# Attention mask: from bf16 matmuls on TensorE to additions by VectorE in PSUM, with the score banks made in the other order

## The chip, the cores and the metric

The kernel runs on one core of one Trainium2 chip. The metric is the device time of one execution, in microseconds (us). The core has TensorE (matmuls, PE in the profile; its weight loads are PEld), VectorE (DVE), ScalarE (ACT), GpSimd (POOL), and SyncE (SP), which issues the transfers here. Each engine works through its own instructions in order and waits on semaphores for the others.

## The reference

A macaron block on x of 4 batches x 1024 tokens x 128 features, all float32: a half-weighted feed-forward (layer norm, gate and up projections, silu, down projection), then attention with 16 heads of 64, then the same feed-forward again. The attention is what matters here:

```
h = silu(x @ W1.T + b1) @ W2.T + b2
q, k, v = split(h @ Wg.T + bg)            # 16 heads of 64
dots = (q @ k.T) * 64 ** -0.5             # per batch and head: 1024 x 1024
mask = j >= i + 64                        # query i sees keys below i + 64
dots = where(mask, -inf, dots)
out = softmax(dots) @ v  ->  @ Wo.T + bo
```

## The kernel before

The two feed-forwards stand at the ends. Between them the attention loop runs 32 turns (`TURNS`): 4 batches by 8 pairs of heads. A turn has 8 steps, c = 0 to 7. Each step handles 128 queries of both heads of the pair ("A" and "B"). The order of the query blocks is written out by hand: `at_step = [0, 7, 2, 6, 1, 5, 3, 4]`. Query block q sees keys 0 to q*128+191, so the widths of the score tiles by step are 192, 1024, 448, 960, 320, 832, 576 and 704: narrow and wide steps alternate.

PSUM has 8 banks of 512 float32 per partition. Banks 0 and 1 hold head A's scores, banks 2 and 3 head B's (`SCORE = (0, 2)`); there is only one such set, so the scores of step c+1 can't be written before both exponentials of step c have read theirs. Banks 4 and 5 take transposed probabilities, bank 6 the attended values and their output projection, bank 7 the projections of q, k and v for this or the next turn.

What one step c does, by engine, in each engine's own order:

- TensorE: `score(c)` (three float32r terms per bank and head; the two heads use two halves of the array); `turns_of(tc, ti, (0, 1))`, the first two groups of transposes of the probabilities of the step three before (`T_LAG = 3`; a group is up to four 128x128 transposes into bank 4 or 5, the even groups into 4, the odd ones into 5); one projection into bank 7 (steps 1 and 2 v, 3 and 4 k, 5 and 6 q); in steps 1, 3, 5 and 7 `attend`, the product with v of a pair of query blocks; in steps 0, 2, 4 and 6 `output`; then transposes of groups 2 and 3; then `masks` of the next step. In steps 0, 4 and 6 there are four groups, in steps 1 and 2 three, elsewhere two or one.
- `masks(c+1)` first waits until both exponentials of step c are done (`exped`, event "B"). It then writes, with bf16 matmuls (`ident16` against a piece of `mask16`), the value -3.0e38 onto the keys that the triangle at the right end of the tile hides, 128 or 64 wide, two matmuls in each step and four in step 6, where the piece crosses a bank. These matmuls open the accumulation group (`start=True`) and `score` adds to it.
- VectorE: `row_max(c)`, one maximum over the row for each head, each waiting for `scored` of its head; `take(tc, 1)`, a copy of transposed group 1 to SBUF; in steps 1 and 2 the copy of v; `take(tc, 3)` where there is a group 3; `invert(c)`, the reciprocal of the sums, which waits for the exponentials; in steps 0, 2, 4 and 6 `add_output`; in steps 3 to 6 `queries_keys_low`, the low part of k or q.
- ScalarE: `take(tc, 0)`, the two exponentials `exps(c)`, `take(tc, 2)`, in steps 1, 3, 5 and 7 `attention_out`, in steps 3 to 6 the high part of k or q (`queries_keys`).
- GpSimd multiplies the probabilities by the reciprocals (`normalise`).

Group 3 of the transposes waits until VectorE has copied group 1 of the same step out of bank 5 (`taken[1]`). The projection in step 4 waits until ScalarE and VectorE have read step 3's from bank 7 (`misc_read`).

Of the kernel before, what the change touches and what calls it, by code (L numbers as in the profile page):

```python
# [13 lines left out]
P = 128  # L14
# [22 lines left out]
def macaron(nc, x, w1t, b1, w2t, b2, wqkvt, bqk, bv, wot, bo, wgatet, wupt, wdownt, out):  # L37
# [37 lines left out]
    DOWN = 0  # L75
    WORK = 7

    def mask_pieces(c):

        lo, hi = at_step[c] * P + WINDOW, width[c]  # L80
        cuts = [lo] + [b for b in (BANK,) if lo < b < hi] + [hi]
        return [(a // BANK, a % BANK, a - lo, b - a) for a, b in zip(cuts, cuts[1:])]

    with ExitStack() as ctx:
        def sb(name, shape, dt=F32):
            return ctx.enter_context(nc.sbuf_tensor(name, shape, dt))
# [2 lines left out]
            return ctx.enter_context(nc.semaphore(name))  # L89

        ident = sb("ident", [P, P])
        ident16 = sb("ident16", [P, P], BF16)
        mask16 = sb("mask16", [P, P], BF16)
        w1_sb = sb("w1_sb", [P, P])
        w2_sb = sb("w2_sb", [P, P])
        b1_sb = sb("b1_sb", [P, 1])
# [61 lines left out]
        def phase(name, lns):  # L158
# [21 lines left out]

        T = lambda n, ev, step=1: Tally(sem(n), ev, step)
        by_head = [f"{c}{h}" for c in range(STEPS) for h in HEADS]
        scored = T("scored", by_head)
        maxed = T("maxed", by_head)
        exped = T("exped", by_head)
        inverted = T("inverted", range(STEPS))
# [14 lines left out]

        credits = {
            "sync": [slots],
            "vector": [maxed, inverted, taken[1], v_done, wo_added, qk_done],
            "scalar": [exped, taken[0], attn_out, qk_high],
            "tensor": [scored, turned, attended, proj, wo_done],
            "gpsimd": [normed],
# [96 lines left out]
        @block.gpsimd  # L304
        def _(pool):
            give_credits(pool, "gpsimd")
            nc.gpsimd.memset(ident[:], 0.0).then_inc(gp_const, 1)
            nc.gpsimd.memset(mask16[:], 0.0).then_inc(gp_const, 1)
            nc.gpsimd.memset(mhalf[:], -0.5).then_inc(gp_const, 1)
            pool.wait_ge(gp_const, 3)  # L310
            nc.gpsimd.affine_select(out=ident[:], in_=ident[:], compare_op=ALU.not_equal, fill=1.0, base=0,
                                    pattern=[[-1, P]], channel_multiplier=1).then_inc(gp_const, 1)

            nc.gpsimd.affine_select(out=mask16[:], in_=mask16[:], compare_op=ALU.is_ge, fill=MASKED, base=-1,
                                    pattern=[[-1, P]], channel_multiplier=1).then_inc(gp_const, 1)
            pool.wait_ge(gp_const, 5)
            nc.gpsimd.tensor_copy(ident16[:], ident[:]).then_inc(gp_const, 1)
            pool.wait_ge(gp_const, 6)

            def rstd_of(ph, ln, t):  # L320
                done(pool, ph.stat[ln], f"a{CT - 1}", t)
                done(pool, ph.norm[ln], "n3", t - 3)
                pool.sem_inc(idle, 1)
                nc.gpsimd.tensor_scalar(veps[ln][:], mv[ln][t % 3][:, :, 1], EPS, None, ALU.add).then_inc(ph.rstd[ln].sem, 1)
                done(pool, ph.rstd[ln], "e", t)
                nc.gpsimd.tensor_tensor(rstd[ln][t % 3][:], veps[ln][:], mhalf[:], ALU.pow).then_inc(ph.rstd[ln].sem, 1)

            def layernorm(ph, t):
                done(pool, ph.rstd["ln1"], "r", t)
                done(pool, ph.tr["ln1"], "t", t - 2)  # L330
                pool.sem_inc(idle, 1)
                for k in range(CT):
                    nc.gpsimd.tensor_scalar(xn["ln1"][t % 2][:, k, :], xres[:, t * CH + k * D:t * CH + (k + 1) * D], mv["ln1"][t % 3][:, k, 0:1],
                                            rstd["ln1"][t % 3][:, k:k + 1], ALU.subtract, ALU.mult).then_inc(ph.norm["ln1"].sem, 1)

            def add_bias(t):
                if t == 0:
                    pool.wait_ge(bo_done, 2)
                done(pool, pa.norm["ln2"], "n3", t)
                here = xres[:, chunk(t)].rearrange("p (k d) -> p k d", d=D)  # L340
                nc.gpsimd.tensor_tensor(here, here, bo_all[:].unsqueeze(1).to_broadcast([P, CT, P]), ALU.add).then_inc(pa.biased.sem, 1)

            def feed_forward(ph):
                for t in range(3):
                    rstd_of(ph, "ln1", t)
                    if t < 2:
                        layernorm(ph, t)
                if ph is pa:
                    for c in range(STEPS):
                        if width[c] < blocks[c] * P:  # L350
                            for h in range(2):
                                nc.gpsimd.memset(probs[c, h][:, width[c]:], 0.0).then_inc(zeroed, 1)
                for t in range(CHUNKS + 2):
                    if ph is pa and 0 <= t - 2 < CHUNKS:
                        rstd_of(pa, "ln2", t - 2)
                    if t + 2 < CHUNKS:
                        layernorm(ph, t + 2)
                    if ph is pa and 0 <= t - 2 < CHUNKS:
                        add_bias(t - 2)
                    if t + 3 < CHUNKS:  # L360
                        rstd_of(ph, "ln1", t + 3)

            feed_forward(pa)

            def normalise(c, i):
                pool.wait_ge(inverted.sem, inverted.after(c, i))
                pool.sem_inc(idle, 1)
                for h in range(2):
                    here = probs[c, h][:, 0:width[c]]
                    nc.gpsimd.tensor_scalar(here, here, recips[:, c, h:h + 1], None, ALU.mult).then_inc(normed.sem, 1)  # L370

            with pool.Fori(0, TURNS) as i:
                for c in range(STEPS):
                    normalise(c, i)

            feed_forward(pd)
# [116 lines left out]
        def _(dve):  # L493
# [75 lines left out]

            def row_max(c, i):  # L570

                for h in range(2):
                    dve.wait_ge(scored.sem, scored.after(f"{c}{HEADS[h]}", i))
                    src = banks[:, SCORE[h]:SCORE[h] + 2, :].rearrange("p b n -> p (b n)")[:, 0:width[c]]
                    nc.vector.tensor_reduce(negmax[:, c, h:h + 1], src, AX.X, ALU.max, negate=True).then_inc(maxed.sem, 1)  # L575

            def invert(c, i):

# [93 lines left out]
        def _(pe):  # L672
# [86 lines left out]
                    if ph is pa and 0 <= t - 2 < CHUNKS:  # L759
                        inner(t - 2)  # L760

            pe.wait_ge(gp_const, 6)
            feed_forward(pa)

            def misc_read(job, n):
# [14 lines left out]
                    last = mm(banks[:, ATTEND, (2 + b) * P:(3 + b) * P], attn[:, j, b * P:(b + 1) * P], w, start=True, stop=True)  # L780
                last.then_inc(wo_done.sem, 1)

            def masks(c, i):

                pe.wait_ge(exped.sem, exped.after(*(lambda t, s: (f"{s}B", t))(*back(i, c, 1))))
                for h in range(2):
                    for b, col, m0, w in mask_pieces(c):
                        mm(banks[:, SCORE[h] + b, col:col + w], ident16[:], mask16[:, m0:m0 + w], start=True, stop=False, skip_group_check=True)  # L788

            def score(c, i, r):  # L790

                masked = {b for b, _, _, _ in mask_pieces(c)}
                if c < 2:
                    pe.wait_ge(qk_done.sem, qk_done.after(("q0", "q1")[c], i))
                edges = list(range(0, width[c], BANK)) + [width[c]]
                for b, (a, z) in enumerate(zip(edges, edges[1:])):
                    terms = ((0, 0), (0, 1), (1, 0))
                    for n, (sq, sk) in enumerate(terms):
                        for h in range(2):
                            last = mm(banks[:, SCORE[h] + b, 0:z - a], qt[r][sq][half(h), at_step[c] * P:(at_step[c] + 1) * P], kt[r][sk][half(h), a:z],  # L800
                                      start=n == 0 and b not in masked, stop=n == 2, skip_group_check=True)
                            if z == width[c] and n == 2:
                                last.then_inc(scored.sem, 1)

            def turn(c, g, i):

# [35 lines left out]
                    if g < groups[c]:  # L842
                        turn(c, g, i)

            def step(c, i, r, carry=True, more=True, final=False):

                ti, tc = back(i, c, T_LAG)
                turning = carry or c >= T_LAG
# [6 lines left out]
                if c in JOBS and runs(job, carry, more):  # L855
                    k = JOB_ORDER.index(job)
                    name, t = (JOB_ORDER[k - 1], i) if k else (JOB_ORDER[-1], i - 1)
                    misc_read(name, job_turn(name, t))
                    project(job, job_turn(job, i), 1 - r if job_turn(job, 0) else r)
                if attending:  # L860
                    attend(ATTEND_AT[c], *((i, r) if c >= PV_LAG else (i - 1, 1 - r)))
                if c in OUTPUTS and runs(OUTPUTS[c], carry, more):
                    output(OUTPUTS[c], job_turn(OUTPUTS[c], i))
                if turning:
                    turns_of(tc, ti, (2, 3))
                if not (final and c == STEPS - 1):
                    n, s = (i, c + 1) if c + 1 < STEPS else (i + 1, 0)
                    masks(s, n)

            pe.wait_ge(pa.h.sem, pa.h.after("h", CHUNKS - 1))  # L870
            pe.wait_ge(pa.x1.sem, pa.x1.after("x", CHUNKS - 1))
            pe.wait_ge(zeroed, 2 * sum(width[c] < blocks[c] * P for c in range(STEPS)))
            pe.wait_ge(qk_done.sem, qk_done.after("k0", 0))
            project("q1", 0, 0, 4)
            masks(0, 0)
            for c in range(STEPS):
                step(c, 0, 0, carry=False)
            with pe.Fori(0, TURNS // 2 - 1) as i2:
# [2 lines left out]
                for c in range(STEPS):  # L881
                    step(c, i2 * 2 + 2, 0)
            for c in range(STEPS):
                step(c, TURNS - 1, 1, more=False, final=True)
            for c in range(PV_LAG):
                if c < T_LAG:
                    turns_of(c + STEPS - T_LAG, TURNS - 1, (0, 1, 2, 3))
# [36 lines left out]
```

## Time and profile before

| what | value |
|---|---|
| time, median of 3 runs | 1389.04 us (1388.59 to 1392.15) |
| the profiled execution's own time | 1391.63 us |
| its span | 1389.7 us |
| granted TensorE clock, mean | 0.993 of full speed |
| TensorE busy | 1346.3 us, 97% |
| VectorE busy | 869.5 us, 63% |
| ScalarE busy | 827.7 us, 60% |
| GpSimd busy | 1041.3 us, 75% |

Busy time is the time covered by an engine's instructions. Matmuls overlap in the records: a 128-column float32 transpose is shown as 279 ns long, and the next starts some 110 ns after it. So the distance between starts, not the length of one, is the price of a matmul among others. In a timeline row with a count, the first number is the start of the first and the second the length of the whole run.

### The profile page before, as it was taken

The page shows a single profiled execution, that of the slowest core. Times are in us where ns is not written, and L with a number is a line of the kernel's source. Part 1 is how long each engine was busy: PE and PEld are TensorE (multiplying, and loading weights), DVE is VectorE, ACT ScalarE, POOL GpSimd, SP SyncE. Part 2 cuts the span into 40 slices and gives each one's busy share as a digit, 9 for nine tenths or more (in the row PEclk, how much of TensorE's full clock was granted, in tenths as well). Part 3 has the DMA queues.
Part 4 walks back from the last instruction along what each step waited for, and adds up shares of the span by engine and source line. Part 5 has one row for each costly group of instructions (what it writes and reads, how often), then busy time and mean ns, then how long its engine had stood idle before and what let it go on. Part 6 is the DMA issues. An engine that isn't in the chain of part 4 may idle for free.

```text
span 1389.7 us, 33797 instructions
## 1 busy us (share of the span) xinstructions
PE 1346.3 (97%) x11538; PEld 1032.1 (74%) x11538; DVE 869.5 (63%) x1726; ACT 827.7 (60%) x1789; POOL 1041.3 (75%) x656
## 2 busy tenths in 40 slices
PE   5978999999999999999999999999999999999988
PEld 4846777777777777777777777777777777777767
DVE  5845666666666666666666666666666666666645
ACT  2435666666666666666666666666666666666532
POOL 6827777777777877778777778777777777778863
PEclk9988999999999999999999999999999999999999
DMA  3100000000000000000000000000000000000001
GB/s 113 43 0 22 22 23 21 21 21 21 3 18 21 21 21 21 21 21 21 21 21 19 2 21 21 21 21 21 21 21 21 21 21 8 13 21 0 1 9 54
DMA packets 31359, 29.47 MB, mean 21 GB/s; under 512 B 7009, under 2 KB 26338, under 8 KB 31330
## 3 DMA queue, kind: packets, MB, share of 16 engines
q1 hardware_dynamic: 31330, 29.09, 6.9%
q8 instruction: 17, 0.28, 0.1%
q14 instruction: 12, 0.10, 0.0%
HBM read 8.07 MB, written 2.10 MB: 7 GB/s over the span
## 4 chain that ended last, share of the span: by engine, by line
PE 93%; DVE 2%; ACT 2%; DMA 1%; issue 1%; POOL 0%; SPq 0%; ACTq 0%; DVEq 0%; POOLq 0%
PE banks L819 24%; PE banks L836 23%; PE banks L800 20%; PE banks L726 9%; PE banks L780 4%; PE banks L730 4%; PE banks L704 3%; PE banks L788 2%; PE banks L696 2%; PE banks L697 2%; DVE kt L595 1%; PE banks L686 1%; ACT probs L440 1%; ACT kt L386 1%; DMA xres<-in_x 1%
## 5 line engine op out<-in xcount | busy, mean ns | idle before, releaser
L370 POOL TENSOR_SCALAR probs<-probs,recips 128x320 f32<-128x320 f32 (+7 forms) x512 | 946.9, 1864 | 281.6 <-DVE recips L580 280.4
L575 DVE TENSOR_REDUCE negmax<-banks 128x1 f32<-128x320 f32 (+7 forms) x512 | 392.8, 809 | 158.7 <-PE banks L800 158.7
L448 ACT ACTIVATE probst<-banks 128x512 f32<-128x512 f32 (+1 forms) x416 | 241.7, 581 | 367.2 <-PE banks L819 363.2
L440 ACT ACTIVATE probs<-banks,negmax 128x320 f32<-128x320 f32 (+7 forms) x512 | 399.1, 784 | 18.5 <-DVE negmax L575 12.2
L819 PE MATMUL banks<-ident,probs 128*128 128x128 f32 x2752 | 389.5, 279 | 3.0 <-DVE probst L587 2.0
L819 PEld LDWEIGHTS banks<-ident,probs 128*128 128x128 f32 x2752 | 297.3, 141 | 66.3 <-issue 53.1
L836 PE MATMUL banks<-probst,vs 128*64 128x128 f32 (+1 forms) x3712 | 326.5, 327 | 0.6 <-DVE xres L613 0.6
L836 PEld LDWEIGHTS banks<-probst,vs 128*64 128x64 f32 x3712 | 231.1, 137 | 121.1 <-issue 52.9
L800 PE MATMUL banks<-kt,qt 64*128 64x512 f32 (+4 forms) x2496 | 299.4, 365 | 0.0
L587 DVE COPY probst<-banks 128x512 f32<-128x512 f32 x320 | 202.2, 632 | 99.7 <-PE banks L819 99.6
L800 PEld LDWEIGHTS banks<-kt,qt 64*128 64x128 f32 x2496 | 206.2, 186 | 46.8 <-issue 0.2
L726 PE MATMUL banks<-hslot,wslot 128*128 128x512 f32 x256 | 136.2, 616 | 1.6 <-ACT h_sb L411 0.8
L440 ACT ACTIVATION_READ_ACCUMULATOR probs<-banks,negmax 128x1 f32 x512 | 101.3, 198 | 0.0
L780 PEld LDWEIGHTS banks<-wo_sb,attn 128*128 128x128 f32 x512 | 72.1, 191 | 29.9 <-issue 29.2
L580 DVE RECIPROCAL recips<-sums 128x2 f32<-128x2 f32 x256 | 41.2, 161 | 83.7 <-ACT probs L440 81.3
L455 ACT ACTIVATE attn<-banks 128x256 f32<-128x256 f32 x128 | 48.9, 382 | 71.6 <-PE banks L836 71.6
L595 DVE SCALAR_TENSOR_TENSOR qt<-banks,bslot,qt 128x512 fp32r<-128x512 f32 x64 | 47.8, 747 | 59.8 <-ACT qt L386 59.8
L780 PE MATMUL banks<-wo_sb,attn 128*128 (+1 forms) x512 | 78.0, 275 | 0.5 <-ACT attn L455 0.5
L788 PE MATMUL banks<-mask,ident 128*128 128x128 bf16 (+1 forms) x576 | 70.2, 213 | 8.1 <-ACT probs L440 8.1
L595 DVE SCALAR_TENSOR_TENSOR kt<-banks,bslot,kt 128x512 fp32r<-128x512 f32 x64 | 47.8, 747 | 47.4 <-ACT kt L386 47.4
L730 PE MATMUL banks<-wslot,hslot 128*128 128x128 f32 x512 | 69.4, 280 | 0.0
L730 PEld LDWEIGHTS banks<-wslot,hslot 128*128 128x128 f32 x512 | 63.7, 196 | 1.0 <-issue 1.0
(59 smaller groups left out, 781.4 us busy)
## 6 DMA issues: line engine op xcount, KB each, us to landing
hslot<-h_sb SPq DMA_DIRECT2D x32, 512.0 KB, 3.2
wslot<-in_wqkvt SPq DMA_DIRECT2D x32, 128.0 KB, 3.0
wslot<-wq_sb SPq DMA_DIRECT2D x32, 64.0 KB, 2.6
y<-xres SPq DMA_DIRECT2D x8, 256.0 KB, 2.3
xres<-in_x SPq DMA_DIRECT2D x2, 256.0 KB, 3.6
wo_sb<-in_wot SPq DMA_DIRECT2D x1, 512.0 KB
wq_sb<-in_wqkvt SPq DMA_DIRECT2D x1, 512.0 KB
bslot<-bqk_sb SPq DMA_DIRECT2D x32, 1.0 KB, 1.9
```

The lines of the kernel that those rows point to most:

```text
L370: nc.gpsimd.tensor_scalar(here, here, recips[:, c, h:h + 1], None, ALU.mult).then_inc(normed.sem, 1)
L440: nc.scalar.activation(probs[c, h][:, 0:width[c]], src, ACT.Exp, bias=negmax[:, c, h:h + 1], accum_out=sums[:, c, h:h + 1]).then_inc(exped ...
L448: nc.scalar.activation(probst[c // 2 % 2][:, 4 * g:4 * g + w, c % 2 * P:(c % 2 + 1) * P], banks[:, TRANSPOSED[g % 2], 0:w * P].rearrange(" ...
L575: nc.vector.tensor_reduce(negmax[:, c, h:h + 1], src, AX.X, ALU.max, negate=True).then_inc(maxed.sem, 1)
L587: nc.vector.tensor_copy(probst[c // 2 % 2][:, 4 * g:4 * g + w, c % 2 * P:(c % 2 + 1) * P], banks[:, TRANSPOSED[g % 2], 0:w * P].rearrange( ...
L595: nc.vector.scalar_tensor_tensor(out=low, in0=banks[:, bank, :], scalar=bslot[r][:, 0:1] if kind == "q" else bslot[r][:, 1:2], in1=high, o ...
L726: last = mm(bank, w, hslot[r][:, j * BANK:(j + 1) * BANK], start=True, stop=True)
L730: last = mm(bank[:, m * P:(m + 1) * P], hslot[r][:, toks], w, start=True, stop=True)
L780: last = mm(banks[:, ATTEND, (2 + b) * P:(3 + b) * P], attn[:, j, b * P:(b + 1) * P], w, start=True, stop=True)
L800: last = mm(banks[:, SCORE[h] + b, 0:z - a], qt[r][sq][half(h), at_step[c] * P:(at_step[c] + 1) * P], kt[r][sk][half(h), a:z], start=n == ...
L819: last = nc.tensor.transpose(banks[:, TRANSPOSED[g % 2], (t - 4 * g) * P:(t - 4 * g + 1) * P], probs[c, h][:, kb * P:(kb + 1) * P], ident[:])
L836: last = mm(banks[half(h), ATTEND, q], vs[r][:, kb, half(h)], probst[p % 2][:, 2 * kb + h, q], start=(kb == 0), stop=(kb == blocks[c1] - 1 ...
```

## The change

The mask matmuls and `mask16`/`ident16` go. A float32 tile `mask` holds the same triangle. `score` now waits itself for the exponentials of the step before, and every bank's first term opens its group. It makes the banks from the last to the first. Where all masked keys lie in the second bank (`EARLY`: steps 1, 3, 5 and 7) it signals `scored` event "m" once the second bank is done, and VectorE adds the mask there, one instruction for each head, while TensorE makes the first bank. In steps 0, 2, 4 and 6 (not `EARLY`) VectorE waits until everything is scored and adds the mask for both heads in one instruction of two blocks. The row maxima wait for the additions (`masked`). In steps with `attend` the transposes of groups 2 and 3 now come ahead of it; that concerns step 1 alone, the only one of them with more than two groups. GpSimd makes no bf16 copy of the identity.

```diff
-    def mask_pieces(c):
-        lo, hi = at_step[c] * P + WINDOW, width[c]
-        cuts = [lo] + [b for b in (BANK,) if lo < b < hi] + [hi]
-        return [(a // BANK, a % BANK, a - lo, b - a) for a, b in zip(cuts, cuts[1:])]
+    hidden_keys = [(q * P + WINDOW, w) for q, w in zip(at_step, width)]
+    EARLY = [lo >= BANK for lo, _ in hidden_keys]
...
-        scored = T("scored", by_head)
+        scored = T("scored", [f"{c}{e}" for c in range(STEPS) for e in ("mAB" if EARLY[c] else "AB")])
+        masked = T("masked", range(STEPS))
...
             def row_max(c, i):
+                lo, hi = hidden_keys[c]
+                rows = banks[:, SCORE[0]:SCORE[0] + 4, :].rearrange("p (h b) n -> p h (b n)", h=2)
+                dve.wait_ge(scored.sem, scored.after(f"{c}m" if EARLY[c] else f"{c}B", i))
+                for heads in ([slice(0, 1), slice(1, 2)] if EARLY[c] else [slice(0, 2)]):
+                    here = rows[:, heads, lo:hi]
+                    hidden = mask[:, 0:hi - lo].unsqueeze(1).to_broadcast([P, here.shape[1], hi - lo])
+                    last = nc.vector.tensor_tensor(here, here, hidden, ALU.add)
+                last.then_inc(masked.sem, 1)
+                dve.wait_ge(masked.sem, masked.after(c, i))
                 for h in range(2):
                     dve.wait_ge(scored.sem, scored.after(f"{c}{HEADS[h]}", i))
-                    src = banks[:, SCORE[h]:SCORE[h] + 2, :].rearrange("p b n -> p (b n)")[:, 0:width[c]]
-                    nc.vector.tensor_reduce(negmax[:, c, h:h + 1], src, AX.X, ALU.max, negate=True).then_inc(maxed.sem, 1)
+                    nc.vector.tensor_reduce(negmax[:, c, h:h + 1], rows[:, h, 0:hi], AX.X, ALU.max, negate=True).then_inc(maxed.sem, 1)
...
-            def masks(c, i):
-                pe.wait_ge(exped.sem, exped.after(*(lambda t, s: (f"{s}B", t))(*back(i, c, 1))))
-                for h in range(2):
-                    for b, col, m0, w in mask_pieces(c):
-                        mm(banks[:, SCORE[h] + b, col:col + w], ident16[:], mask16[:, m0:m0 + w], start=True, stop=False, skip_group_check=True)
             def score(c, i, r):
-                masked = {b for b, _, _, _ in mask_pieces(c)}
+                n, s = back(i, c, 1)
+                pe.wait_ge(exped.sem, exped.after(f"{s}B", n))
...
-                for b, (a, z) in enumerate(zip(edges, edges[1:])):
+                parts = list(enumerate(zip(edges, edges[1:])))
+                for k, (b, (a, z)) in enumerate(reversed(parts)):
...
-                                      start=n == 0 and b not in masked, stop=n == 2, skip_group_check=True)
-                            if z == width[c] and n == 2:
+                                      start=n == 0, stop=n == 2, skip_group_check=True)
+                            if n == 2 and k == len(parts) - 1:
                                 last.then_inc(scored.sem, 1)
+                    if EARLY[c] and k == 0:
+                        last.then_inc(scored.sem, 1)
...
             def step(c, i, r, carry=True, more=True):
...
+                if turning and attending:
+                    turns_of(tc, ti, (2, 3))
                 if attending:
                     attend(ATTEND_AT[c], *((i, r) if c >= PV_LAG else (i - 1, 1 - r)))
...
-                if turning:
+                if turning and not attending:
                     turns_of(tc, ti, (2, 3))
-                if not (final and c == STEPS - 1):
-                    n, s = (i, c + 1) if c + 1 < STEPS else (i + 1, 0)
-                    masks(s, n)
```

## Rows read from the trace of the kernel before

**Rows 1.** The page: span, busy time by engine, the ending chain by line.

```profile
span 1389.7 us, 33797 instructions
...
PE 1346.3 (97%) x11538; PEld 1032.1 (74%) x11538; DVE 869.5 (63%) x1726; ACT 827.7 (60%) x1789; POOL 1041.3 (75%) x656
...
PE banks L819 24%; PE banks L836 23%; PE banks L800 20%; PE banks L726 9%; PE banks L780 4%; PE banks L730 4%; PE banks L704 3%; PE banks L788 2%; PE banks L696 2%; PE banks L697 2%; DVE kt L595 1%; PE banks L686 1%; ACT probs L440 1%; ACT kt L386 1%; DMA xres<-in_x 1%
```

**Rows 2.** The page's groups: count | busy us, mean ns | idle before.

```profile
L788 PE MATMUL banks<-mask,ident 128*128 128x128 bf16 (+1 forms) x576 | 70.2, 213 | 8.1 <-ACT probs L440 8.1
```

**Rows 3.** Timeline of TensorE over one turn: start us, length us, instructions.

```profile
634.73 0.58 PE L800 MATMUL banks<-kt,qt 64*128 64x192 f32 x6
...
636.62 0.94 PE L819 MATMUL banks<-ident,probs 128*128 128x128 f32 x6
...
637.39 0.23 PE L788 MATMUL banks<-mask,ident 128*128 128x64 bf16 x2
637.55 1.66 PE L800 MATMUL banks<-kt,qt 64*128 64x512 f32 x12
...
643.38 0.44 PE L819 MATMUL banks<-ident,probs 128*128 128x128 f32 x2
643.65 0.27 PE L788 MATMUL banks<-mask,ident 128*128 128x128 bf16 x2
...
643.86 0.88 PE L800 MATMUL banks<-kt,qt 64*128 64x448 f32 x6
...
654.98 0.30 PEld L726 LDWEIGHTS banks<-hslot,wslot 128*128 128x128 f32 x2 [0.21 <-DVE kt L595]
...
656.38 1.04 PE L819 MATMUL banks<-ident,probs 128*128 128x128 f32 x8
...
663.24 1.22 PE L800 MATMUL banks<-kt,qt 64*128 64x512 f32 x12
...
666.62 1.04 PE L819 MATMUL banks<-ident,probs 128*128 128x128 f32 x8
...
667.70 1.28 PE L800 MATMUL banks<-kt,qt 64*128 64x512 f32 x12
...
672.68 0.58 PE L800 MATMUL banks<-kt,qt 64*128 64x192 f32 x6
```

**Rows 4.** Timeline of VectorE over the same turn.

```profile
635.34 0.62 DVE L575 TENSOR_REDUCE negmax<-banks 128x1 f32<-128x192 f32 x2 [1.05 <-PE banks L800]
...
654.84 0.88 DVE L575 TENSOR_REDUCE negmax<-banks 128x1 f32<-128x320 f32 x2
...
655.64 0.68 DVE L587 COPY probst<-banks 128x512 f32<-128x512 f32 x1
...
664.80 1.41 DVE L575 TENSOR_REDUCE negmax<-banks 128x1 f32<-128x576 f32 x2
...
666.13 0.68 DVE L587 COPY probst<-banks 128x512 f32<-128x512 f32 x1
...
667.69 0.69 DVE L587 COPY probst<-banks 128x512 f32<-128x512 f32 x1 [0.89 <-PE banks L819]
...
669.35 1.68 DVE L575 TENSOR_REDUCE negmax<-banks 128x1 f32<-128x704 f32 x2
```

**Rows 5.** Timeline of ScalarE over the same turn.

```profile
636.42 0.42 ACT L440 ACTIVATE probs<-banks,negmax 128x192 f32<-128x192 f32 x1
...
661.95 0.20 ACT L440 ACTIVATION_READ_ACCUMULATOR probs<-banks,negmax 128x1 f32 x1
...
671.84 0.20 ACT L440 ACTIVATION_READ_ACCUMULATOR probs<-banks,negmax 128x1 f32 x1
```

**Rows 6.** Line L613: VectorE's PSUM plus SBUF addition, min/median/max ns.

```profile
L613 DVE TENSOR_TENSOR xres<-banks,xres x100: 402/405/425, 305.3 to 1246.5; 128x256 f32 x100
```

**Rows 7.** Timeline of the last turn, step 6: VectorE, then TensorE.

```profile
1310.18 0.68 DVE L587 COPY probst<-banks 128x512 f32<-128x512 f32 x1
...
1311.01 0.63 PE L819 MATMUL banks<-ident,probs 128*128 128x128 f32 x4 [0.21 <-DVE probst L587]
```

More of the change, by code:

```diff
@@ L91, in macaron @@
         ident = sb("ident", [P, P])
-        ident16 = sb("ident16", [P, P], BF16)
-        mask16 = sb("mask16", [P, P], BF16)
+        mask = sb("mask", [P, P])
         w1_sb = sb("w1_sb", [P, P])
@@ L203, in macaron @@
             "sync": [slots],
-            "vector": [maxed, inverted, taken[1], v_done, wo_added, qk_done],
+            "vector": [masked, maxed, inverted, taken[1], v_done, wo_added, qk_done],
             "scalar": [exped, taken[0], attn_out, qk_high],
@@ L307, in _ @@
             nc.gpsimd.memset(ident[:], 0.0).then_inc(gp_const, 1)
-            nc.gpsimd.memset(mask16[:], 0.0).then_inc(gp_const, 1)
+            nc.gpsimd.memset(mask[:], 0.0).then_inc(gp_const, 1)
             nc.gpsimd.memset(mhalf[:], -0.5).then_inc(gp_const, 1)
@@ L312, in _ @@
                                     pattern=[[-1, P]], channel_multiplier=1).then_inc(gp_const, 1)
-            nc.gpsimd.affine_select(out=mask16[:], in_=mask16[:], compare_op=ALU.is_ge, fill=MASKED, base=-1,
+            nc.gpsimd.affine_select(out=mask[:], in_=mask[:], compare_op=ALU.is_ge, fill=MASKED, base=-1,
                                     pattern=[[-1, P]], channel_multiplier=1).then_inc(gp_const, 1)
             pool.wait_ge(gp_const, 5)
-            nc.gpsimd.tensor_copy(ident16[:], ident[:]).then_inc(gp_const, 1)
-            pool.wait_ge(gp_const, 6)
             def rstd_of(ph, ln, t):
@@ L760, in feed_forward @@
                         inner(t - 2)
-            pe.wait_ge(gp_const, 6)
+            pe.wait_ge(gp_const, 5)
             feed_forward(pa)
@@ L843, in turns_of, with step @@
                         turn(c, g, i)
-            def step(c, i, r, carry=True, more=True, final=False):
+            def step(c, i, r, carry=True, more=True):
                 ti, tc = back(i, c, T_LAG)
@@ L874, in _ @@
             project("q1", 0, 0, 4)
-            masks(0, 0)
             for c in range(STEPS):
@@ L883, in _ @@
             for c in range(STEPS):
-                step(c, TURNS - 1, 1, more=False, final=True)
+                step(c, TURNS - 1, 1, more=False)
             for c in range(PV_LAG):
```

## The prediction

> **What bounds the kernel now.** I read the page first, then the ending chain, then the timelines of one turn engine by engine. TensorE is busy 97% of the span, VectorE 63%, and the chain that ends last is nearly all TensorE lines [rows 1]. The mask matmuls are 576 instructions (18 a turn) with 70.2 us of records, and they waited only 8.1 us for the exponentials [rows 2]. So today the wait for ScalarE costs almost nothing, and dropping the masks looks like a gain of up to 5%. Two things shrink that. First, records of matmuls overlap, so 70.2 us is no price; the distances between starts are. Second, the chain score, maximum, exponential, next score has a fixed length in each step, and so has the one through group 1's copy to group 3's transposes. I therefore take one turn, 634.73 to 672.68, 37.95 us from score to score [rows 3], and go through its eight steps, asking what ends last in each once the masks are gone and the additions are in.
>
> **What a mask piece costs TensorE.** Before step 2 the second of two transposes starts at 643.38 + 0.44 - 0.28 = 643.54 (the run less one record, front matter), the first mask at 643.65, the score at 643.86 [rows 3]: 0.32 us from transpose to score, 0.21 of it from mask to score. The most that can be saved is 0.21. The second mask starts about 0.06 after the first, and the score 0.15 after that; a transpose's record is 0.06 longer than a mask's, so the worst case leaves 0.22 of the 0.32 and saves 0.10. I take 0.17, nearer the upper end because the two slots are surely gone. Eight such boundaries would be 1.4 us a turn, 44 us in 32 turns. TensorE changes from full-array transposes or half-column `attend` to the half-row score tiles as often as before. The Trainium skill, TensorEngine Tiling (Array Packing), Key Properties, says that a change of tiling mode drains TensorE; by that rule alone the masks' own slots are saved and the drain stays, which is the 0.10 end. The trace shows the 0.15 gap after the masks but can't say what the gap after a transpose is.
>
> **What an addition costs VectorE.** In the kernel before VectorE never writes to PSUM. The nearest row is L613, PSUM plus SBUF into SBUF, 128x256: 405 ns [rows 6]. The copy of 128x512 takes 0.68 [rows 4], so an element costs (680 - 405) / 256 = 1.07 ns and the fixed part is about 0.13 us. The addition of steps 0, 2, 4 and 6 (2 x 128) is then 0.41; one head's 128 columns are 0.27, and 64 columns 0.20. Waiting for its own end before the maximum adds 0.03 (estimate: below it nothing, above it the 0.15 of TensorE's resume after a copy, below). Where the addition comes in the way, the maxima start 0.44 later in those four steps, and in steps 5 and 7, where two follow each other and overlap by some 0.08, 0.20 + 0.28 + 0.03 = 0.51 later. Bounds: from below, an addition with its fixed part hidden, 0.28; from above, the fixed part doubled, 0.56. All additions together are 32 x (4 x 0.41 + 6 x 0.27 + 2 x 0.20) = 117 us, which takes VectorE to about 71%: no bound by itself.
>
> **Step by step.** "Gain" is how much earlier the next score starts than before.
>
> Step 0. The maxima began at 635.34, two in 0.62 [rows 4]; the first exponential began only at 636.42, behind ScalarE's copy [rows 5]. With the addition the second maximum ends at 635.34 + 0.44 + 0.62 = 636.40. The exponentials are not later. The last of six transposes starts at 636.62 + 0.94 - 0.28 = 637.28, the mask at 637.39 and score 1 at 637.55 [rows 3]. The exponentials end at about the same time as the transposes, so score 1 can't start ahead of 637.39: gain 0.10 instead of 0.17.
>
> Steps 1 to 3. In 1 and 3 VectorE idles ahead of the maxima, so the early additions lie beside the first bank's matmuls and cost nothing; were that idle time gone, each pair would push the exponentials by 0.5. Step 2 has no group 3, and its exponentials wait for ScalarE's copy about as long as for the addition. Moving group 2 ahead of `attend` in step 1 is free: the copy it waits for is over by then. Gain 0.17 at scores 2 and 3. At score 4 it is 0.17 too, but the projection of step 4 already waits 0.21 for VectorE's low part of k [rows 3], which hangs on `attend` of step 3 through ScalarE. What TensorE gains after that `attend` it waits out there: 0.
>
> Step 4. The maxima come right behind that low part, at 654.84, and the copy of group 1 at 655.64 [rows 4]. With 0.44 more the copy ends at 655.64 + 0.44 + 0.68 = 656.76. In the last turn, TensorE resumes 0.15 after such a copy: the copy ends at 1310.86 and group 3 starts at 1311.01 [rows 7]. So group 3 starts at 656.91 where it started at 656.38 + 4 x 0.11 = 656.82 [rows 3]. Gain at score 5: 0.17 - 0.10 = 0.07.
>
> Step 5. VectorE is occupied right up to the maxima, so the two additions push the exponentials by 0.51 and the late copies by some 0.1 more. They ended at 662.15 [rows 5], 1.09 ahead of score 6 at 663.24 [rows 3]; less 0.17 and 0.6 that still leaves some 0.3. Nothing lost. With `attend` of step 5 the turn stands 0.10 + 0.17 + 0.17 + 0.07 = 0.51 ahead.
>
> Step 6. From here I count against the end of that `attend`, since VectorE's low part of q hangs on it. The maxima began behind it, at 664.80, and the copy of group 1 at 666.13 [rows 4]. That copy now ends at 666.13 + 0.44 + 0.68 = 667.25, group 3 starts at 667.40 instead of 666.62 + 0.44 = 667.06 [rows 3], 0.34 later. Score 7 starts at about 667.9 instead of 667.70.
>
> Step 7. The copy of group 3 went at 667.69 as soon as the transposes were there [rows 4], and the reciprocal, the output and the low part of q stand between it and the maxima at 669.35, without a gap. All move by 0.34, and the two additions add 0.51: 0.85. The exponentials ended at 672.04 [rows 5], now 672.89, and 0.06 later score 0 starts, at 672.95, where it was 672.68 [rows 3]: 0.27 lost, while TensorE idles.
>
> **The sum.** 0.51 - 0.27 = 0.24 us a turn, 32 x 0.24 = 7.7 us. The head, the feed-forwards and GpSimd's dropped copy give nothing that is seen. The profiled execution took 1391.6 with a span of 1389.7 [rows 1], 2.6 over the median of 1389.0; from its own time I get 1383.9, for the median 1381.3. Of the 44 us that the masks seem to be worth, most goes into waits for VectorE in steps 4, 6 and 7. What is late next is the last exponential of step 7; score 0 waits for it, and the copies and exponentials of step 0 come as much later.
>
> **Rivals.**
> *Slower, because an addition into PSUM is dearer.* Where the chain decides, each addition's extra time is paid: once in steps 0 and 4, and three times up to score 0 (once through step 6's copy, twice in step 7). So x more per addition costs 5x a turn, and the gain is gone at x = 0.24 / 5 = 0.05 us. With the fixed part doubled (x = 0.13 to 0.15) the turn is some 0.5 longer than before, 16 us: 1405; at 0.10 it is 1397. For it: no row shows VectorE writing to PSUM, and the threshold is small. Against it: 402 to 425 ns is all that L613 needs [rows 6], with a read from PSUM in it. The Trainium skill, Perfetto Trace Analysis, Optimizing Scalar/DVE Operations, gives VectorE some 60 ns of access overhead on SBUF and 125 on PSUM. As an estimate from that page, an output in PSUM may take 65 ns more, which by the 5x would make 1392; no row of this case shows it.
> *Much faster: the additions are covered.* If neither group 1's copies nor the exponentials ever end last, the gain is 0.10 + 6 x 0.17 = 1.12 a turn (score 4's is lost in any case), 36 us: 1353. Additions 0.10 shorter would already give back 0.10 in step 4 and 0.30 up to score 0: 0.64 a turn, 20 us, 1369. Against it: VectorE has no gap in steps 6 and 7 to hide them in [rows 4].
> *No change: the boundary is worth only 0.10.* Then the gains are 0.05 + 0.10 + 0.10 + 0 and the loss of 0.27 stays, since it hangs on VectorE: 0 to 1 us, 1389.
>
> **Chances and range.** What I forecast 0.40, with its own range of 1375 to 1386; slower by the addition 0.27; covered 0.18; no change 0.15. A measurement of this kernel tells about 0.3%, 4.2 us, from no change. Faster: 0.38 of my own case and 0.18 of the covered one, 0.56. Same: 0.13 of the third rival, 0.02 of mine, 0.04 from the weak end of the slower one, 0.19. Slower: 0.25. The range for 8 in 10 reaches from 1358, most of the way to full cover, to 1402, an addition about 0.13 longer.
>
> **What the new profile would show.** The L788 groups gone and TensorE's records 70 us less; a new VectorE addition, 12 a turn, 384 in all, 0.41 for the wide ones; VectorE at about 985 us busy. In a turn: transposes waiting for the copy in steps 4 and 6 (0.1 and 0.3 us), score 0 waiting 0.3 for the exponential of step 7, the projection in step 4 waiting some 0.35, and 37.7 us from score to score. Wide additions over 0.46 would make me wrong toward slower. A score that starts 0.11 after the last transpose, or exponentials in step 7 that end ahead of `attend`, would make me wrong toward faster.

## The result

The changed kernel takes 1399.15 us in the median of four runs (1397.15 to 1402.75), the kernel before 1389.87 in the same comparison. The ratio is 1.0064, 95% interval 1.0043 to 1.0085: slower by 6 to 12 us, where 1381.3 and faster was forecast. The time lies inside the stated range and near the first rival's 1397.

The page of the changed kernel: span, busy time, the ending chain by engine and by line, and three groups (count | busy us, mean ns | idle before, and what ended it).

```profile
span 1395.2 us, 33649 instructions
...
PE 1323.9 (95%) x10962; PEld 980.4 (70%) x10962; DVE 976.6 (70%) x2110; ACT 827.3 (59%) x1789; POOL 1040.7 (75%) x655
...
PE 70%; DVE 13%; issue 9%; ACT 5%; DVEq 1%; DMA 1%; ACTq 0%; POOL 0%; SPq 0%; POOLq 0%
...
L822 PE MATMUL banks<-ident,probs 128*128 128x128 f32 x2752 | 402.5, 281 | 14.3 <-DVE probst L593 13.6
...
L801 PE MATMUL banks<-kt,qt 64*128 64x512 f32 (+4 forms) x2496 | 303.2, 369 | 18.6 <-ACT probs L437 18.6
...
L576 DVE TENSOR_TENSOR banks<-banks,mask 128x128 f32<-128x128 f32 (+2 forms) x384 | 113.5, 326 | 78.9 <-PE banks L801 77.9
```

The chain by engine on the page of the kernel before, to be laid beside it:

```profile
PE 93%; DVE 2%; ACT 2%; DMA 1%; issue 1%; POOL 0%; SPq 0%; ACTq 0%; DVEq 0%; POOLq 0%
```

TensorE has 576 matmuls less and 22 us less busy time, and yet the span is 5.5 us longer. The chain that was nearly all TensorE now has 13% VectorE and 9% "issue" in it. The additions are there, 384 of them, 113.5 us. Transposes wait 13.6 us for VectorE's copies and scores 18.6 us for exponentials; the second replaces the 8.1 us that the masks waited [rows 2].

One turn of TensorE (start us, length us), to be laid beside [rows 3]:

```profile
635.76 0.58 PE L801 MATMUL banks<-kt,qt 64*128 64x192 f32 x6 [0.27 <-ACT probs L437]
...
638.61 1.65 PE L801 MATMUL banks<-kt,qt 64*128 64x512 f32 x12
...
644.64 0.88 PE L801 MATMUL banks<-kt,qt 64*128 64x448 f32 x6
...
648.25 1.55 PE L801 MATMUL banks<-kt,qt 64*128 64x448 f32 x12
...
653.71 0.71 PE L801 MATMUL banks<-kt,qt 64*128 64x320 f32 x6
...
655.62 1.13 PE L732 MATMUL banks<-hslot,wslot 128*128 128x512 f32 x2 [0.18 <-DVE kt L601]
...
658.15 1.39 PE L801 MATMUL banks<-kt,qt 64*128 64x320 f32 x12
...
663.68 1.30 PE L801 MATMUL banks<-kt,qt 64*128 64x64 f32 x12
...
668.10 0.66 PE L822 MATMUL banks<-ident,probs 128*128 128x128 f32 x4 [0.35 <-DVE probst L593]
668.68 1.30 PE L801 MATMUL banks<-kt,qt 64*128 64x192 f32 x12
...
673.90 0.58 PE L801 MATMUL banks<-kt,qt 64*128 64x192 f32 x6 [0.36 <-ACT probs L437]
```

The differences between the starts of the scores give a table. "Predicted" is the length before less or plus what the prediction gave each step; the last column is an experiment below.

| from score to score | before | predicted | changed | e11, waits swapped |
|---|---|---|---|---|
| 0 to 1 | 2.82 | 2.72 | 2.85 | 2.75 |
| 1 to 2 | 6.31 | 6.14 | 6.03 | 6.06 |
| 2 to 3 | 3.72 | 3.55 | 3.61 | 3.61 |
| 3 to 4 | 5.70 | 5.53 | 5.46 | 5.47 |
| 4 to 5 | 4.18 | 4.28 | 4.44 | 4.37 |
| 5 to 6 | 5.78 | 5.61 | 5.53 | 5.53 |
| 6 to 7 | 4.46 | 4.83 | 5.00 | 4.90 |
| 7 to 0 | 4.98 | 5.05 | 5.22 | 5.13 |
| the turn | 37.95 | 37.71 | 38.14 | 37.82 |

The turn is 0.19 us longer, 6 us in 32, which is what the two profiled executions differ by (5.5). Over 31 turns, from the first score 0 to the last, a turn is 38.06 us before and 38.26 changed, 0.20 longer, so the one turn stands for the others. It should have been 0.24 shorter. Steps 0, 4, 6 and 7 miss: they are 0.13, 0.16, 0.17 and 0.17 longer than forecast, 0.63 together; the other four are 0.20 shorter together. In 4, 6 and 7 the prediction let VectorE's chain end last. In step 0 it did not, and what ends last there is VectorE's copy of group 1, which starts 1.74 us after score 0 (637.50) where it started 1.64 after it; the weight load for group 3 waits 0.21 for this copy, and the six transposes take 1.03 instead of 0.94 [rows 3]. First the copy before, then copy and transposes of the changed kernel:

```profile
636.37 0.69 DVE L587 COPY probst<-banks 128x512 f32<-128x512 f32 x1 [0.40 <-PE banks L819]
...
637.50 0.68 DVE L593 COPY probst<-banks 128x512 f32<-128x512 f32 x1
...
637.64 1.03 PE L822 MATMUL banks<-ident,probs 128*128 128x128 f32 x6
```

The reason can be read on VectorE, steps 6 and 7, beside [rows 4], with ScalarE's last exponential of step 7 beneath:

```profile
665.47 0.42 DVE L576 TENSOR_TENSOR banks<-banks,mask 128x256 f32<-128x256 f32 x1
666.02 1.42 DVE L581 TENSOR_REDUCE negmax<-banks 128x1 f32<-128x576 f32 x2
667.36 0.68 DVE L593 COPY probst<-banks 128x512 f32<-128x512 f32 x1
668.79 0.69 DVE L593 COPY probst<-banks 128x512 f32<-128x512 f32 x1 [0.75 <-PE banks L822]
...
670.45 0.49 DVE L576 TENSOR_TENSOR banks<-banks,mask 128x128 f32<-128x128 f32 x2
671.06 1.69 DVE L581 TENSOR_REDUCE negmax<-banks 128x1 f32<-128x704 f32 x2
```

```profile
673.55 0.20 ACT L437 ACTIVATION_READ_ACCUMULATOR probs<-banks,negmax 128x1 f32 x1
```

The addition ends at 665.89 and the maximum starts at 666.02, 0.13 later, where 0.03 was allowed. The maxima are pushed by 0.55 instead of 0.44, and by 0.61 instead of 0.51 behind a pair. The rest follows in the forecast order: the copy ends at 668.04 and group 3 starts behind it at 668.10; the last exponential ends at 673.75 and score 0 starts at 673.90. The two gaps, 0.06 and 0.15, were forecast the other way round, 0.15 and 0.06, and cancel. The ending chain of the changed kernel shows what lies in those 0.13 us (start, length, what; DVEq is VectorE's queue):

```profile
665.47 0.43 DVE banks L576
665.90 0.03 issue
665.93 0.04 DVEq L580
665.97 0.05 issue
666.02 0.09 DVE negmax L581
```

L580 is the code line of the maximum's wait for its scores, which stands behind the wait for the addition. The trace has an arithmetic instruction of VectorE's queue at this line, and the semaphore that this instruction waits for is the one that the addition raises; the maximum itself waits for the semaphore of the scores, which has long been met. So the late wait sits one instruction ahead of the maximum: the addition ends, the queue's instruction runs (0.04), and only then is the maximum issued. 240 of the 256 first maxima in this trace have that instruction right in front of them.

### The profile page after: what moved, and what is told of

The parts are those of the page before. It is cut to its first block, busy times and chain, and to the rows that moved or that the text cites. A ratio compares the mean times of both kernels' runs of the same rounds, so it can differ in the third digit from the quotient of the medians.

```text
span 1395.2 us, 33649 instructions
## 1 busy us (share of the span) xinstructions
PE 1323.9 (95%) x10962; PEld 980.4 (70%) x10962; DVE 976.6 (70%) x2110; ACT 827.3 (59%) x1789; POOL 1040.7 (75%) x655
## 4 chain that ended last, share of the span: by engine, by line
PE 70%; DVE 13%; issue 9%; ACT 5%; DVEq 1%; DMA 1%; ACTq 0%; POOL 0%; SPq 0%; POOLq 0%
PE banks L822 18%; PE banks L839 16%; PE banks L801 14%; PE banks L732 6%; DVE negmax L581 4%; PE banks L736 4%; PE banks L786 3%; PE banks L710 3%; DVE banks L576 2%; PE banks L702 2%; PE banks L703 2%; DVE qt L601 2%; ACT probs L437 2%; DVE kt L601 2%; DVE probst L593 2%
## 5 line engine op out<-in xcount | busy, mean ns | idle before, releaser
L581 DVE TENSOR_REDUCE negmax<-banks 128x1 f32<-128x320 f32 (+7 forms) x512 | 394.0, 811 | 39.9 <-PE banks L801 17.4
L822 PE MATMUL banks<-ident,probs 128*128 128x128 f32 x2752 | 402.5, 281 | 14.3 <-DVE probst L593 13.6
L801 PE MATMUL banks<-kt,qt 64*128 64x512 f32 (+4 forms) x2496 | 303.2, 369 | 18.6 <-ACT probs L437 18.6
L801 PEld LDWEIGHTS banks<-kt,qt 64*128 64x128 f32 x2496 | 193.9, 187 | 79.9 <-issue 36.1
L576 DVE TENSOR_TENSOR banks<-banks,mask 128x128 f32<-128x128 f32 (+2 forms) x384 | 113.5, 326 | 78.9 <-PE banks L801 77.9
```

The costliest lines, as they stand in the source:

```text
L581: nc.vector.tensor_reduce(negmax[:, c, h:h + 1], rows[:, h, 0:hi], AX.X, ALU.max, negate=True).then_inc(maxed.sem, 1)
L822: last = nc.tensor.transpose(banks[:, TRANSPOSED[g % 2], (t - 4 * g) * P:(t - 4 * g + 1) * P], probs[c, h][:, kb * P:(kb + 1) * P], ident[:])
```

## The experiments

First theory: VectorE's chain, longer by more than forecast, takes what TensorE gains, and the excess is the wait of the maxima for VectorE's own result. Rivals: the reorderings cost it; the output in PSUM does; VectorE's load does. Each ratio below is to runs of the kernel before on the same chip, with its 95% interval.

**e1: what the masks are worth.**

```diff
-                dve.wait_ge(scored.sem, scored.after(f"{c}m" if EARLY[c] else f"{c}B", i))
-                for heads in ([slice(0, 1), slice(1, 2)] if EARLY[c] else [slice(0, 2)]):
...
-                dve.wait_ge(masked.sem, masked.after(c, i))
```

> The changed kernel with no mask at all: no additions, no mask matmuls, so every query also attends to the hidden keys in its tile (that part of the computation is left out). Own theory (the masks are worth their boundary on TensorE, and the additions on VectorE's chain took more than that): each boundary gives 0.2 to 0.28 us as seen at scores 2 and 6 of the changed kernel, except score 1 (0.10, the exponentials end there) and score 4 (lost at the projection): 1.2 to 1.4 us a turn less than before, 1345 to 1352. Rival (the boundary is worth only its two matmul slots, 0.10): 1370 to 1375.

1358.33 us, ratio 0.9768 (0.9748 to 0.9788): between the two, so neither expectation was met. A turn is 36.93, 1.02 less than before. Three rows of TensorE:

```profile
651.37 1.04 PE L811 MATMUL banks<-ident,probs 128*128 128x128 f32 x8
652.34 1.29 PE L792 MATMUL banks<-kt,qt 64*128 64x192 f32 x12
...
657.12 0.58 PE L792 MATMUL banks<-kt,qt 64*128 64x192 f32 x6
```

The last transpose starts at 651.37 + 1.04 - 0.28 = 652.13 and score 7 at 652.34: 0.21, where before it was 667.38 to 667.70 [rows 3], 0.32. So behind transposes the masks are worth 0.11. Behind `attend` they are worth more: score 7 to score 0 takes 4.78 here, 4.98 before. The clean comparison is with e2 below, which has e1's order of banks and transposes and keeps the masks: the four scores behind `attend` (2, 4, 6 and 0) come 6.26, 5.69, 5.75 and 5.00 us after the score ahead of them in e2 and 6.05, 5.48, 5.54 and 4.78 in e1, 0.21 or 0.22 less each. The 0.17 of the prediction is about the mean of two different prices. Masks away, with nothing in their place, is 32 us; the additions then cost 41.

**e2: the two reorderings alone**, in the kernel before.

```diff
-                for b, (a, z) in enumerate(zip(edges, edges[1:])):
+                for b, (a, z) in reversed(list(enumerate(zip(edges, edges[1:])))):
...
+                if turning and attending:
+                    turns_of(tc, ti, (2, 3))
```

> The kernel before, mask matmuls and all, with the change's two reorderings alone: banks of the scores from last to first, and in step 1 the transposes of group 2 ahead of attend. Own theory: neither matters, 1389 within 0.3%. Rival (the bank order makes the scores signal later, or the moved transposes hold up attend): 1394 or more, that is at least half of what the change lost.

1391.73 us, ratio 1.0007 (0.9997 to 1.0017). Neither matters in sum: against the kernel before, step 1 is 0.05 shorter, steps 6 and 7 are 0.08 and 0.02 longer. The first rival falls.

**e3 and e4: the output and the wait apart.** In e3 the additions write to a spare SBUF tile, so the mask isn't applied; e4 also drops the wait.

```diff
-                    last = nc.vector.tensor_tensor(here, here, hidden, ALU.add)
+                    spare = (y1, x2t)[c % 2][:].rearrange("p (h n) -> p h n", h=2)[:, heads, 0:hi - lo]
+                    last = nc.vector.tensor_tensor(spare, here, hidden, ALU.add)
...
-                dve.wait_ge(masked.sem, masked.after(c, i))        # e4 only
```

> The changed kernel, but the additions write their sums into a spare SBUF tile, so the mask is not applied; the wait of the maxima for the additions stays. Own theory (the wait of VectorE for its own result is what costs, and the output in PSUM only some 0.02 us): additions of 0.41 instead of 0.43, the maxima still start 0.12 after their end, 5 x 0.02 = 0.1 us a turn less, 1394 to 1398. Rival (writing to PSUM is what costs, also by holding up the maximum that reads there): near the 1381 predicted for the change.

> As e3_spare_wait, mask not applied, but the maxima do not wait for the additions, which they no longer read. Own theory: the maximum starts about 0.08 before the addition's end instead of 0.12 after it, 0.20 us less in each step; steps 0, 4, 6 and 7 hand it on, 0.7 to 0.8 us a turn less than e3: 1372 to 1378. Rival (the wait costs nothing beyond 0.03, the price lies in the output): same as e3 within 5 us.

e3: 1396.94 us, ratio 1.0047 (1.0030 to 1.0064). e4: 1374.71 us, 0.9885 (0.9864 to 0.9906). The same additions without a wait behind them are 22 us cheaper. Written to SBUF instead of PSUM they are at most some 2 us cheaper, which isn't shown to differ from nothing: the interval of e3 overlaps that of the changed kernel (1.0043 to 1.0085). In e4 the maxima of step 6 start 0.33 after the addition, and in the changed kernel 0.55:

```profile
658.34 0.41 DVE L577 TENSOR_TENSOR y<-banks,mask 128x256 f32<-128x256 f32 x1
658.67 1.41 DVE L581 TENSOR_REDUCE negmax<-banks 128x1 f32<-128x576 f32 x2
```

The rival of the output falls: e3's wide additions take 420 ns in the mean, those of the changed kernel 428.

**e5: one addition for each head, each maximum waiting for its own.**

```diff
-                for heads in ([slice(0, 1), slice(1, 2)] if EARLY[c] else [slice(0, 2)]):
+                for heads in (slice(0, 1), slice(1, 2)):
...
-                    last = nc.vector.tensor_tensor(here, here, hidden, ALU.add)
-                last.then_inc(masked.sem, 1)
-                dve.wait_ge(masked.sem, masked.after(c, i))
+                    nc.vector.tensor_tensor(here, here, hidden, ALU.add).then_inc(masked.sem, 1)
                 for h in range(2):
                     dve.wait_ge(scored.sem, scored.after(f"{c}{HEADS[h]}", i))
+                    dve.wait_ge(masked.sem, masked.after(f"{c}{HEADS[h]}", i))
```

> The changed kernel, mask applied as there, but one addition for each head in every step and each maximum waits for its own head's addition alone, so head B's addition runs while the wait for head A's goes by. Own theory: the maxima start about 0.41 to 0.45 after the first addition's start instead of 0.55 (wide) and 0.61 (pairs of step 7), some 0.5 us a turn less: 1380 to 1386. Rival (what costs is the time VectorE is occupied by additions, and a fifth instruction of fixed length adds to it): not below 1397.

1375.18 us, ratio 0.9894 (0.9867 to 0.9921): 24 us less than the changed kernel, with 128 additions more. Better than expected, because the maxima start 0.39 after the first addition, ahead of the second one's end (657.75), so the wait for the first is hidden behind the second:

```profile
657.26 0.49 DVE L576 TENSOR_TENSOR banks<-banks,mask 128x128 f32<-128x128 f32 x2
657.65 1.41 DVE L580 TENSOR_REDUCE negmax<-banks 128x1 f32<-128x576 f32 x2
```

VectorE is busy 70% of the span as in the changed kernel (966.6 us against 976.6), so load is not the cause.

**e6 to e10: in which steps additions cost.** The mask stays a matmul in the steps of `BY_MATMUL`; the bf16 mask tile serves both. With "by head", additions and waits are e5's.

```diff
+    BY_MATMUL = (0, 2, 4, 6, 7)        # e6; e7 (0, 4, 6, 7) and e8 (4, 6, 7), by head; e9 (6, 7); e10 (4, 6), by head
...
+                if c in BY_MATMUL:
+                    for h in range(2):
+                        for b, col, m0, w in mask_pieces(c):
+                            opened.add(b)
+                            mm(banks[:, SCORE[h] + b, col:col + w], ident16[:], mask[:, m0:m0 + w], start=True, stop=False, skip_group_check=True)
```

> Additions only in steps 1, 3 and 5, whose maxima have slack; the mask stays a matmul (made at the head of the scores) in steps 0, 2, 4, 6 and 7. The mask tile is bf16 for both. Own theory (additions cost only where VectorE's chain ends last): the boundaries ahead of scores 1, 3 and 5 give 0.07 to 0.12 us each, nothing is handed on: 1378 to 1383. Rival (VectorE's load as such slows the turn): 1389 or more.

> As e6 with additions also in step 2 and none in step 0, one for each head with its own wait. Own theory: the boundary ahead of score 2 stands behind attend and gives 0.24 more, step 2 hands on at most 0.05: 1371 to 1377, faster than both kernels. Rival: as e6 or slower.

> As e7 with additions in step 0 too (so matmul masks in 4, 6 and 7 alone). Own theory: score 0 stands behind attend and gives 0.2, and step 0's additions delay its exponentials by 0 to 0.1: 1366 to 1373. Rival (step 0's chain already ends last, so its additions cost what the boundary gives): same as e7.

> The changed kernel with the mask as a matmul in steps 6 and 7 alone (one wide addition in 0, 2 and 4, pairs in 1, 3 and 5, as there). Own theory: the two long steps from score 6 to score 0 (5.00 and 5.22 us in the changed kernel, 4.46 and 4.98 before) come back, 0.78 us a turn, less 0.24 for the mask matmuls ahead of score 6: 0.5 a turn, 1380 to 1385. Rival (every addition costs alike): a third of the additions gone, 1394 to 1397.

> As e8, with additions in step 7 too (matmul masks in 4 and 6 alone), one for each head with its own wait. Own theory: the boundary ahead of score 7 gives 0.11, and 0.40 more ahead of step 7's maxima just uses up the 0.42 of slack that its exponentials had, so 0 to 3 us less than e8: 1368 to 1373. Rival (step 7 hands on what it gets, as in the changed kernel): 3 us or more above e8.

| run | additions in steps | us | ratio to before |
|---|---|---|---|
| e6 | 1, 3, 5 | 1381.03 | 0.9936 (0.9915 to 0.9957) |
| e7 | 1, 2, 3, 5, by head | 1375.50 | 0.9895 (0.9872 to 0.9917) |
| e8 | 0, 1, 2, 3, 5, by head | 1372.01 | 0.9876 (0.9852 to 0.9900) |
| e9 | 0 to 5 | 1376.09 | 0.9898 (0.9877 to 0.9920) |
| e10 | all but 4 and 6, by head | 1372.27 | 0.9880 (0.9854 to 0.9906) |

All five are faster than both kernels, by 0.6% to 1.2% against the kernel before. e9 says where the change fails: with matmuls in steps 6 and 7 alone it is 23 us faster than with additions there too. Its turn starts and ends at these scores, 37.51 apart:

```profile
629.86 0.58 PE L817 MATMUL banks<-kt,qt 64*128 64x192 f32 x6
...
662.59 1.29 PE L817 MATMUL banks<-kt,qt 64*128 64x192 f32 x12
...
667.37 0.58 PE L817 MATMUL banks<-kt,qt 64*128 64x192 f32 x6
```

It came out below its 1380 to 1385: step 7 takes 4.78 to score 0, not the 4.98 reckoned with, since the mask ahead of score 0 stays gone. e8 and e10 can't be told apart in time. In their traces the boundary ahead of score 7 gives 0.11 (4.43 us from score 6 in e10, 4.54 in e8), and step 7's additions by head hand on 0.20 to score 0 (4.99 against 4.79): they use up the slack and a little more.

**e11 and e12: the order of two waits.**

```diff
-                dve.wait_ge(masked.sem, masked.after(c, i))
                 for h in range(2):
                     dve.wait_ge(scored.sem, scored.after(f"{c}{HEADS[h]}", i))
+                    if h == 0:
+                        dve.wait_ge(masked.sem, masked.after(c, i))
                     nc.vector.tensor_reduce(negmax[:, c, h:h + 1], rows[:, h, 0:hi], AX.X, ALU.max, negate=True).then_inc(maxed.sem, 1)
```

> The changed kernel with two waits of VectorE in the other order and nothing else: the maximum's wait for its scores (long met) first, then the one for the addition. In the trace of the changed kernel the wait for the scores is an instruction of its own on VectorE's queue, carried out only after the addition has ended, 0.13 us from addition to maximum. Theory (that queued instruction is what costs; the wait for its own result is 0.03 as between two other VectorE groups of the kernel before): the maxima start 0.03 after the addition, 0.09 less in each step, four to five times a turn, 1383 to 1389, near the prediction. Rival (0.13 is the time VectorE's own result takes to be seen by it): unchanged within 0.3%.

> e5_by_head with the two waits of each maximum in the changed kernel's order, that for the addition first and that for the scores behind it (e5 had them the other way round). Tells how much of e5's gain came from the order and how much from splitting the additions. Theory of the queued instruction: 0 to 0.09 us later maxima than e5's 0.40, up to 0.4 us a turn, 1375 to 1388. Rival (splitting alone hides the wait): as e5, 1375 within 0.3%.

e11: 1385.34 us, ratio 0.9964 (0.9950 to 0.9978), 1.0% under the changed kernel's ratio. Nothing is changed but that the wait already met is asked first. The queue's instruction, now at L581, waits for the scores and runs at 665.44, ahead of the addition; the maximum itself waits for the addition. The addition ends at 666.06 and the maximum starts at 666.10; over all 128 wide additions the gap is 0.035 us in the median, where it is 0.122 in the changed kernel. So the rival, that 0.13 is what VectorE's own result takes to be seen, falls. The waits of TensorE shrink with the gap:

```profile
665.64 0.42 DVE L576 TENSOR_TENSOR banks<-banks,mask 128x256 f32<-128x256 f32 x1
666.10 1.42 DVE L582 TENSOR_REDUCE negmax<-banks 128x1 f32<-128x576 f32 x2
```

```profile
636.07 0.58 PE L802 MATMUL banks<-kt,qt 64*128 64x192 f32 x6 [0.18 <-ACT probs L437]
...
668.18 0.66 PE L823 MATMUL banks<-ident,probs 128*128 128x128 f32 x4 [0.25 <-DVE probst L594]
...
673.89 0.58 PE L802 MATMUL banks<-kt,qt 64*128 64x192 f32 x6 [0.28 <-ACT probs L437]
```

e12: 1379.16 us, ratio 0.9914 (0.9898 to 0.9931), against e5's 0.9894 (0.9867 to 0.9921): the intervals overlap. Once head B's addition covers the gap, the order of the waits has little left to cost. The splitting alone is thus worth 1.5% against the changed kernel, with the order 1.7%.

## Why the prediction was wrong

**The step that failed** is the term "waiting for its own end before the maximum adds 0.03". It measured 0.13, and e11 shows what the other 0.10 was: not the time in which VectorE sees its own result, which is the 0.03 to 0.04 assumed, but the queue's instruction that the second wait puts between the addition and the maximum. The prediction looked at the addition and the wait for it, and not at the wait for the scores that follows it in the code. With the additions' 0.42 to 0.43 for 0.41, the push was 0.55 for 0.44 and 0.61 for 0.51. Swapping the waits takes the turn from 38.14 to 37.82, 0.32 of the 0.43 by which it missed the forecast, and brings the ratio below 1. No experiment isolates the 0.11 that remains; the boundaries behind transposes, 0.11 instead of 0.17, are part of it.

**The first rival's lever was right in size, and the extra time decided the sign.** The first rival had it that every addition's extra time is paid five times a turn and that 0.05 us uses up the gain. The extra time was 0.11, which by that rule is 0.55 a turn, from 0.24 gained to 0.31 lost, 1399; measured was 1399.15. That this meets the median is partly luck: the turn lost 0.19 and not 0.31, because four steps are 0.20 shorter than forecast, and one of the five additions that count, step 0's, counts through a copy that the rule didn't have. Its reason was wrong: it blamed the write into PSUM, which e3 puts at 8 ns in an addition and at most some 2 us in all. The prediction's estimate of 65 ns more for an output in PSUM, from the Trainium skill, Perfetto Trace Analysis, Optimizing Scalar/DVE Operations, isn't borne out for this instruction, which reads PSUM in both kernels: 428 ns with the output in PSUM, 420 with it in SBUF.

**What TensorE gains.** In sum right: forecast 0.17 a boundary, measured 0.11 behind transposes and 0.21 to 0.22 behind `attend` (e1 against e2). The prediction was wrong that TensorE changes its mode "as often as before". Behind transposes it does: the masks are full-array like them. Behind `attend` the rows show 128*64 matmuls, then 128*128 masks, then 64*128 scores, two changes, where one is left without the masks. The rule of the Trainium skill, TensorEngine Tiling (Array Packing), Key Properties, that a change of mode drains the engine, so puts the 0.10 end behind transposes alone and a larger gain behind `attend`; the traces agree with both (0.11, and 0.21 to 0.22), though no run separates the drain from the masks' own slots. Step 1 gained more than forecast because the moved transposes put `attend` right ahead of score 2.

**Step 4.** Score 4's gain was lost at the projection as forecast: TensorE waits there in the changed kernel and in e1 alike, and the projection starts 1.91 and 1.92 us after score 4, where it was 1.70.

**Step 0.** The exponentials are not later, as forecast: the first begins 1.70 us after score 0, 1.69 before. The copy of group 1, which also stands behind the maxima, is later, and group 3 waits for it. The prediction asked this question in steps 4 and 6 and not here. With the waits swapped the step takes 2.75, near the forecast 2.72.

**Steps 6 and 7.** Right in mechanism: group 3 waits for the late copy (0.35 us), score 0 for the last exponential (0.36). Forecast were 0.3 each. One thing more is in step 6: its scores take 1.23 to 1.24 us to the next transposes instead of 1.15, in the changed kernel and in e1 and e2, that is with the reversed banks alone.

**The odd steps.** Additions in 1, 3 and 5 cost nothing, as forecast (e6). In step 5 it was closer than forecast: in the changed kernel the exponentials end 0.11 us ahead of score 6 (663.57 and 663.68), where some 0.3 was to be left.

**What stays open.** The medians differ by 9 us and the profiled executions by 5.5, with 0.19 a turn in the turn read. The rest goes with TensorE's mean granted clock. The four executions of the changed kernel had 0.988 to 0.993 of full speed, and the one at 0.988 was the longest (1402.75). The kernel before, in the runs for the experiments, had 0.991 to 0.996. At 0.993 it took 1391.8 to 1392.9 us in ten executions, against 1398.11 for the changed kernel: 5 to 6 us. Why the changed kernel was granted less isn't shown.

## What to carry to other kernels

Where a unit's result feeds the same unit's next instruction, count every wait between the two, not only the one on the result: put the waits that are met already first and the late one last (1.0% here), or put other work in the gap, such as the second head's addition (1.5% by itself, 1.7% with the order). Before work is moved from the bound engine to one with 37% idle time, mark the steps in which that engine ends the chain, by every result that others wait for (copies as well as maxima): the move pays in the steps with slack (e8, 1.2% faster than before) and loses in the others. A forecast whose sign hangs on 0.05 us in an unseen sequence should bound the whole sequence as the code issues it.

## What the hardware showed that was not expected

With the late wait first, 0.09 us was lost each time although the other had long been met (0.12 to 0.13 from result to use in that order, 0.03 to 0.04 in the other). Removing a bf16 matmul pair of full-array mode ahead of half-row matmuls saved 0.11 us behind transposes and 0.21 to 0.22 behind half-column matmuls.
